# One sublayer of a Trainium2 kernel, a gated delta rule over 64 units: where its corner, join, output and keys products stand in the instruction order

## The reference, cut to what matters

```python
def step(S, inp):
    qt, kt, vt, at, bt = inp
    err = jnp.einsum('bhvk,bhk->bhv', S, kt) - vt
    S = at[..., None, None] * S - bt[..., None, None] * err[..., None] * kt[:, :, None, :]
    o = jnp.einsum('bhvk,bhk->bhv', S, qt)
    return (S, o)
...
q = _silu(_dwconv_causal(x @ Wq, conv_q_w, conv_q_b))
k = _silu(_dwconv_causal(x @ Wk, conv_k_w, conv_k_b))
v = _silu(_dwconv_causal(x @ Wv, conv_v_w, conv_v_b))
...
o = (o - mu) * jax.lax.rsqrt(var + 1e-05) * ln_w + ln_b
o = (o * jax.nn.sigmoid(x @ Wg).reshape(B, T, H, DV)).reshape(B, T, H * DV)
return o @ Wo
```

## Time and profile before

| | |
|---|---|
| three runs | 3297.91, 3301.82, 3304.41 us; median 3301.82 |
| the profiled execution, its own time | 3297.91 us |
| its span in the profile | 3295.8 us |
| busy share of the span | PE 97%, PEld 80%, DVE 73%, ACT 59%, POOL 25% |
| the changed loop | about 488 to 1918 us of the span |

### The profile page before, as it was taken

The page is one execution under the profiler, slowest core; times in us unless marked ns, Lnnn a source line. Parts: engine busy times, 40 slices in busy tenths (PEclk is TensorE's granted clock), DMA queues, the critical chain, the costliest instruction groups (busy, mean ns, idle before and its releaser), DMA issues. The chain is left out here.

```text
span 3295.8 us, 89322 instructions
## 1 busy us (share of the span) xinstructions
PE 3187.0 (97%) x34218; PEld 2636.1 (80%) x34218; DVE 2411.4 (73%) x7923; ACT 1952.9 (59%) x4769; POOL 828.0 (25%) x828
## 2 busy tenths in 40 slices
PE   8999989999999999999999969999899999999999
PEld 6888878888888888888888857888777777777787
DVE  5777778787778878787877647777766777777764
ACT  3565556666666666666666625555565556555653
POOL 2333322232223323222222223333300111111100
PEclk9999999999999999999999989999999999999999
DMA  6000000000000000000000040000000000000000
GB/s 245 1 1 1 1 14 21 22 22 19 21 12 25 18 25 19 22 15 22 22 22 21 9 165 1 1 1 1 1 1 1 2 1 1 1 5 4 5 8 11
DMA packets 51337, 66.83 MB, mean 20 GB/s; under 512 B 4962, under 2 KB 40291, under 8 KB 49379
## 3 DMA queue, kind: packets, MB, share of 16 engines
q1 hardware_dynamic: 49330, 60.21, 5.7%
q10 hardware_dynamic: 1584, 0.93, 0.1%
HBM read 58.56 MB, written 2.56 MB: 19 GB/s over the span
## 5 line engine op out<-in xcount | busy, mean ns | idle before, releaser
L1433 DVE SCALAR_TENSOR_TENSOR d_acc<-d_raw,d_taps,d_acc 128x255 f32<-128x255 f32 x1116 | 623.7, 600 | 128.9 <-ACT d_raw L1421 115.7
L2496 ACT ACTIVATE s_probs<-s_probs,s_nmax 128x128 f32<-128x128 f32 (+1 forms) x768 | 286.9, 446 | 176.1 <-DVE s_nmax L202 175.4
L1688 ACT COPY d_power<-bank 128x768 f32<-128x768 f32 x320 | 259.1, 810 | 135.1 <-PE bank L1681 135.1
L202 DVE CUSTOM_DVE_ANT_0 s_probs<-bank,mask 128x128 f32<-128x128 f32 (+1 forms) x768 | 225.4, 348 | 101.9 <-PE bank L2477 101.9
L736 POOL TENSOR_TENSOR a_q<-a_rope 64x512 f32<-64x512 f32 x128 | 165.9, 1296 | 527.5 <-DVE a_recip L806 312.9
L773 ACT ACTIVATE a_area<-a_area,a_nmax 128x128 f32<-128x128 f32 (+1 forms) x512 | 226.4, 443 | 87.8 <-DVE a_nmax L202 87.1
L1419 ACT ACTIVATE d_acc<-bank,d_tap_bias,d_taps 128x256 f32<-128x256 f32 x372 | 189.9, 561 | 148.4 <-PE bank L1397 138.6
L202 DVE CUSTOM_DVE_ANT_0 a_area<-bank,mask 128x128 f32<-128x128 f32 (+1 forms) x512 | 158.6, 355 | 131.9 <-PE bank L754 127.1
L801 ACT COPY a_area<-bank 128x512 f32<-128x512 f32 (+1 forms) x260 | 137.2, 581 | 111.6 <-PE bank L792 111.6
L726 DVE TENSOR_TENSOR a_rope<-bank,a_sinT 32x512 f32<-32x512 f32 x256 | 177.4, 693 | 5.6
L1836 POOL TENSOR_TENSOR d_o_rs<-d_o_var,minus_half 128x4 f32<-128x4 f32 x64 | 69.5, 1087 | 419.3 <-DVE d_o_var L1830 419.3
(11 more groups left out here) (287 smaller groups left out, 8640.1 us busy)
## 6 DMA issues: line engine op xcount, KB each, us to landing
d_alpha<-d_alpha_rows SPq DMA_DIRECT2D x64, 256.0 KB, 3.6
d_g_decay<-d_running_rows SPq DMA_DIRECT2D x32, 258.0 KB, 3.5
a_w_o<-in_a_w_o SPq DMA_DIRECT2D x2, 2048.0 KB, 16.8
a_area<-in_a_q_nope SPq DMA_DIRECT2D x2, 1536.0 KB, 9.2
x<-in_x SPq DMA_DIRECT2D x8, 256.0 KB, 15.0
d_wk<-in_d_wk SPq DMA_DIRECT2D x1, 2048.0 KB
d_wq<-in_d_wq SPq DMA_DIRECT2D x1, 2048.0 KB
d_wv<-in_d_wv SPq DMA_DIRECT2D x1, 2048.0 KB
```

The costliest lines, as they stand in the source:

```text
L202: return core.nc.vector.tensor_tensor_reduce(out=out, in0=scores, in1=core.mask[:, blocks], scale=-1.0, scalar=HIGHEST, op0=ALU.add, op1=A ...
L1433: last = nc.vector.scalar_tensor_tensor(out=convolved(G, r)[:, j, d:T], in0=raw[:, r % 2, j, 0:T - d], scalar=taps[:, r // 2, h, 3 - d:4 - ...
L1688: nc.scalar.copy(power[:], b_step[:, :, 0:3 * P]).then_inc(g.step_out, 1)
L2496: last = nc.scalar.activation(own, own, ACT.Exp, scale=-1.0, bias=nmax[:, s % 2, t, i:i + 1])
```

## The change

The corner of unit e = u - 1 is no longer issued at the end of unit e but at the start of u, just ahead of doubling 0 of u. `out_pe` of e - 1 and `kk_pe` of u + 1 follow, then `join_pe` of e, doubling 1 of u, and `y_pe` of e, which stood ahead of `kk_pe`. The corner is written to the banks of the join (`b_join`) instead of the fourth column block of `b_step`, and corner and join count on semaphores of their own, so a unit's doublings count six steps instead of eight. ACT's order follows: corner copy, doubling 0, [ab], sigmoid, join copy, doubling 1, y copy. `out_pe` of the last unit follows the loop.

```diff
-STEPS = LEVELS + 2
+STEPS = LEVELS
...
         def corner_pe(pe, u):
             pe.wait_ge(g.step_out, STEPS * u + LEVELS)
+            need(pe, g.y_ready, u)
+            need(pe, g.oT_affine, u)
+            need(pe, g.rhs_ready, (u + 1) // 2 if u % 2 == 1 else 0)
...
-            last.then_inc(g.step_in_psum, 1)
+            last.then_inc(g.close_in_psum, 1)
...
         def y_pe(pe, e):
-            pe.wait_ge(g.step_out, STEPS * (e + 1))
+            pe.wait_ge(g.close_out, 2 * (e + 1))
...
             @block.tensor
+                    if e >= 0:
+                        corner_pe(pe, e)
                     if live:
                         step_pe(pe, u, 0)
-                    if e >= 0:
-                        y_pe(pe, e)
+                    if e >= 1:
+                        out_pe(pe, e - 1)
                     if u + 1 < UNITS:
                         kk_pe(pe, u + 1)
                     if n == CHUNKS - 2 and u + 2 < UNITS:
                         ab_pe(pe, u // CHUNKS + 1)
+                    if e >= 0:
+                        join_pe(pe, e)
                     if live:
                         step_pe(pe, u, 1)
+                    if e >= 0:
+                        y_pe(pe, e)
                     if q is not None:
                         project_pe(pe, q)
...
                         qk_pe(pe, u)
-                        corner_pe(pe, u)
                     if q is not None:
                         project_pe(pe, q + 3)
-                    if e >= 0:
-                        out_pe(pe, e)
                     if n == CHUNKS - 3 and u + 3 < UNITS:
                         xnT_pe(pe, u // CHUNKS + 1, q + 4)
-                    if live:
-                        join_pe(pe, u)
+                out_pe(pe, UNITS - 1)
...
             @block.scalar
+                    if e >= 0:
+                        corner_act(act, e)
                     if live:
                         step_act(act, u, 0)
-                    if e >= 0:
-                        y_act(act, e)
+                    if n == CHUNKS - 2 and u + 2 < UNITS:
+                        ab_act(act, u // CHUNKS + 1)
                     if odd and ahead is not None:
                         sigmoid_act(act, ahead, 2)
                     if not odd and u < UNITS:
                         sigmoid_act(act, G, 5)
-                    if n == CHUNKS - 2 and u + 2 < UNITS:
-                        ab_act(act, u // CHUNKS + 1)
+                    if e >= 0:
+                        join_act(act, e)
                     if live:
                         step_act(act, u, 1)
+                    if e >= 0:
+                        y_act(act, e)
```

More of the change, by code:

```diff
@@ L1210, in __init__ @@
         self.step_in_psum, self.step_out = sem("d_step_in_psum"), sem("d_step_out")
+        self.close_in_psum, self.close_out = sem("d_close_in_psum"), sem("d_close_out")
         self.y_in_psum, self.y_ready = sem("dy_in_psum"), sem("dy_ready")
@@ L1526, in n_act @@
             act.wait_ge(g.n_in_psum, u + 1)
-            need(act, g.step_in_psum, STEPS * (u - 2) + LEVELS + 1)
+            need(act, g.close_in_psum, 2 * (u - 2) + 1)
             nc.scalar.copy(wide(n0[u % 2][:]), b_kk[:, :]).then_inc(g.n_ready, 1)
@@ L1630, in step_pe @@
                 pe.wait_ge(g.n_ready, u + 1)
-            need(pe, g.step_out, STEPS * u + l if l > 0 else STEPS * u - 1)
+            need(pe, g.step_out, STEPS * u + l)
             lo_a = 2 * P
@@ L1724, in join_pe, with corner_act @@
                 cols = half(pair)
+                nc.tensor.matmul(b_join[half(c), 0, cols], tT[half(0), u % 2, j, half(0)],
+                                 core.ident[half(0), half(0)], start=True, stop=True,
+                                 tile_position=(0, c * HALF), skip_group_check=True)
+                last = nc.tensor.matmul(b_join[half(c), 1, cols], n0[u % 2][half(1), j, half(0)],
+                                        tT[half(1), u % 2, j, half(1)], start=True, stop=True,
+                                        tile_position=(HALF, c * HALF), skip_group_check=True)
+            last.then_inc(g.close_in_psum, 1)
+        def corner_act(act, u):
+            act.wait_ge(g.close_in_psum, 2 * u + 1)
+            nc.scalar.copy(corner[:], b_join[:, :, 0:P]).then_inc(g.close_out, 1)
+        def join_pe(pe, u):
+            pe.wait_ge(g.close_out, 2 * u + 1)
+            for j in range(GH):
+                pair, c = j // 2, j % 2
+                cols = half(pair)
                 last = nc.tensor.matmul(b_join[half(0), c, cols], corner[half(c), 0, cols],
@@ L1727, in join_pe @@
                                         tile_position=(c * HALF, 0), skip_group_check=True)
-            last.then_inc(g.step_in_psum, 1)
+            last.then_inc(g.close_in_psum, 1)
         def join_act(act, u):
-            act.wait_ge(g.step_in_psum, STEPS * (u + 1))
+            act.wait_ge(g.close_in_psum, 2 * (u + 1))
             heads = tT[half(0), u % 2, :, half(1)].rearrange("p (q s) t -> p s q t", s=2)
             nc.scalar.copy(heads, b_join[half(0), :, 0:P].rearrange("p s (q t) -> p s q t", q=2))\
-                .then_inc(g.step_out, 1)
+                .then_inc(g.close_out, 1)
         def y_pe(pe, e):
             c = e % 2
-            pe.wait_ge(g.step_out, STEPS * (e + 1))
+            pe.wait_ge(g.close_out, 2 * (e + 1))
             if c == 0:
@@ L2040, in _ @@
                         sigmoid_act(act, ahead, 4 if odd else 1)
[L2041 to L2044, removed]
+                    if live and not odd:
+                        k_act(act, u)
                     if q is not None:
@@ L2048, in _ @@
                         xnT_act(act, u // CHUNKS + 1, q + 4)
-                    if live:
-                        join_act(act, u)
             @block.gpsimd
```

## The result

The changed kernel took **3322.18 us** (median of 4 runs, 3319.81 to 3324.74) against 3299.86 us for the kernel before on the same chip (4 runs, 3295.77 to 3304.41): a ratio of 1.0067, with a 95% interval of 1.0050 to 1.0085. It is slower by 22 us. The prediction said 3320, slower, by +19.2 us. The profiled execution took 3319.81 us, 21.90 more than that of before.

The account below looks back on a forecast made before the run. PE was taken to bound the loop, at work all but 7 of 1360 us. The terms, 22.7 - 10.2 + 6.9 + 3.1 - 3.3 = +19.2 us, gave 3317 or 3321; it said 3320, range 3304 to 3334.

Parts of the forecast that it names:

- The 0.34 a unit: PE, from qk to the end of the round behind doubling 1: 10.92 us before, 10.58 after, one quarter group fewer.
- By the drain alone: PE's tiling mode changes: without the load that isn't prefetched, each unit would gain 0.24 us and the sum be 3 higher.
- kk waits for the keys: PE's kk waits for DVE's keys, 1.2 us in most odd units, 1.7 in a sequence's last; odd halves sum to 22.7.
- the yw pairs: Odd units where state had waited for yw before: state +0.32 us, 7 of them.
- The last pair of a sequence: State +0.99 us in its odd unit, input's wait 0.99, y's wait for the join copy 0.45, seven times; PE-bound half -0.34.
- The input's wait: xnT_pe, now directly behind the last round, waits for ACT's copy: 0.99 us, 7 times, 6.9 us.
- The end: Units 62 and 63: y fills doubling 2's wait for ACT and the corner no longer delays out: -3.3 us.
- The first odd unit: First odd unit that projects: its keys are early, so -0.2 us.
- Free keys: Rival: the keys don't hold kk up, and the gain lands until yw stops it; 3295 us, chance 0.09.
- Corner and join free in company: Rival: keys hold kk up, but corner's 0.24 and join's 0.25 cost nothing beside the doublings; 3299 us, chance 0.08.
- ACT is late for y: Rival: ACT's join copy is late in every unit, y 0.3 us later 61 times; 3338 us, chance 0.08.
- waits and order together: Rival: nothing changes, PE keeps its work and waits merely change place; 3302 us, chance 0.04.

Follow-up runs that it names:

- All three: Changed kernel with second half of keys ahead of pT, next sequence's input transposes behind doubling 0 of the seventh unit, kk behind doubling 1: 3271.85 us, ratio 0.9912.
- keys first: Changed kernel with DVE making the second half of the keys ahead of pT instead of behind it: 3287.61 us, ratio 0.9956 to the kernel before.
- old keys: Changed kernel whose kk of an even unit reads the previous group's keys without waiting for DVE (wrong output): 3296.88 us, ratio 0.9982 to the kernel before.
- before, keys first: Kernel before the change, with DVE making the second half of the keys ahead of pT: 3310.92 us, ratio 1.0027.

## Why the prediction was right

**The 0.34 a unit.** Right, 0.32 measured. The changed kernel shows it itself in an even unit, where nothing is late. From qk to the doubling behind the next round (doubling 2) it takes:

```profile
1072.29 1.06 PE L1597 MATMUL bank<-d_qT,d_kT 128*128 128x128 f32 x8
...
1083.00 0.25 PE L1641 MATMUL bank<-d_signs,ident_bf 64*64 64x128 bf16 x4
```

10.71 us, and in the kernel before:

```profile
1061.72 1.06 PE L1596 MATMUL bank<-d_qT,d_kT 128*128 128x128 f32 x8
...
1072.75 0.25 PE L1640 MATMUL bank<-d_signs,ident_bf 64*64 64x128 bf16 x4
```

11.03. The terms in company are near too: corner and doubling 0 take 1.26 in the odd unit shown above (1051.98 to 1053.24; 1.23 in the prediction), join and doubling 1 take 1.10 (1057.41 to 1058.51; 1.10). "All three" agrees with 0.83 and 0.84 a pair, against 0.89 from the prediction's terms. By the drain alone, 0.24 in the prediction, a pair would have gained 2 x 0.24 + 0.21 = 0.69. The rows lie nearer to 0.34, as the prediction had chosen, and still don't say which part is the drain and which the load. kk starts 2.05 behind out in "keys first", where its weights wait for the keys, and 1.83 where they don't: keys that are just late cost 0.22 there, their load and their lateness together.

**kk waits for the keys.** Right in place and size: 36.3 us over 31 units against "35 to 42 us in all" over 30 (35.2 without the first odd unit). The ordinary pairs grew by 0.41 and 0.51 against 0.86 - 0.34 = 0.52, the yw pairs by -0.03 against -0.02.

**The last pair of a sequence** was sized at 0.99 + 0.99 + 0.45 - 0.34 = 2.09 and measured 1.89. The input's wait was sized at 0.99 and measured 1.01; y's was sized at 0.45 and measured 0.36. The 0.13 left is in the keys' term, 0.99, if the 0.34 is taken as it stands.

**The end.** Sized at -3.3, measured -3.10 over the last pair.

**The first odd unit.** Sized at -0.2 and measured -0.22, for a reason that did not hold. State stands at 516.00 against 515.41 before, but this execution entered the loop at the lower clock: its first kk took 1.96 us instead of 1.16. Counted from the round behind that, state comes 23.53 us later (492.47 to 516.00) against 23.75 before (491.66 to 515.41). The prediction had the keys early there. They were not: kk waited 1.07 us in this unit as well. What made up for it is that the corner and y, which had waited 0.30 and 0.59 us for ACT in the first unit before, no longer did. That the size fits is luck.

**Not in the prediction:** the two clock falls, 3.3 us. From first to last state the prediction's steps make 19.4 (the sum without the first unit), and 20.67 - 3.3 = 17.4 was measured without the falls. That the total came out so near is luck in part, by two small errors of opposite sign: the ordinary pairs, where 7 of 16 grew by 0.41 instead of 0.52, and the last pairs with 1.89 instead of 2.09 had been sized some 2 us too high, and the falls were missing.

**A detail that went otherwise.** The prediction left open what GpSimd's product for the queries would fall on. It fell on the decay scan, which takes 2.40 us beside it, against 1.36 in the kernel before, where the product fell on the taps behind (3.59 us; now 2.70). The collision moved, and the sum on DVE stayed nearly the same. The scan and the taps both read two SBUF operands. The Trainium skill (SBUF — State Buffer, Who interferes with whom) says that such an instruction of DVE shares its second read with a GpSimd instruction that reads SBUF; the trace agrees, with 2.40 against 1.36 for the scan and 3.59 against 2.70 for the taps. "Keys first" moved part of the product's time onto pT, whose first operand comes from PSUM: pT keeps its 1.12, and the scan falls to 1.69 in the unit shown above, and to between 1.36 and 1.40 in other odd units.

**The rivals.** Free keys (3295) was the closest to what "old keys" made of the kernel, 3297. Corner and join free in company would have left doubling 0 with the corner, and doubling 1 with the join, 0.24 and 0.25 shorter than the 1.26 and 1.10 that they took, and "all three" as much shorter in each unit. ACT is late for y in seven units and in no others. And waits and order together changed every kind of pair but one.

## What to carry to other kernels

An order that saves time on the busiest engine also brings its next reader forward; before making such a change, walk each operand of the moved stretch back to where it is made, for the saving is paid out only as far as the first operand that is not ready. Then ask which work now stands behind that wait that used to fill the time ahead of it: it comes on top, and here it turned a saving of 0.9 us a pair into a loss of about 0.5. One swap of two instructions on another engine, worthless and even harmful by itself, turned the loss of 0.7% into a gain of 0.4%; with two more covers it became 0.9%. When one piece of a reordering looks harmful, look first at what the pieces cover for each other: putting out back without the corner that had hidden part of its wait made the kernel slower still.

## What the hardware showed that I had not expected

A wait of 0.3 us behind a stretch of small products, in a loop that is otherwise at the full clock, was followed by half clock in 11 of 42 cases, at about 1.65 us each, five times the wait itself. The decay scan stands 0.20 us when it directly follows pT on the same engine ("keys first" and "before, keys first", and some even units of the kernel before as well, as at 618.3); with the keys' product between the two, that stall is not there (1056.18, no wait). A semaphore from DVE was seen by PE 0.06 us after the record of its instruction ended.
